# An attention kernel on one core: six products for the row maxima of a unit become four, and they are issued in another order

## What is computed

```python
qkv = (x @ w_qkv.T).reshape(B, N, 3, H, hd).transpose(2, 0, 3, 1, 4)   # 8 heads, hd = 24, g = 8
q3, q4, q5 = (q[..., :g], q[..., g:2 * g], q[..., 2 * g:])             # k and v the same way
x3 = merge(_attn(q4, concatenate([k3, k4], axis=2), concatenate([v3, v4], axis=2), scale))
x4 = merge(_attn(q5, concatenate([k3, k5], axis=2), concatenate([v3, v5], axis=2), scale))
x5 = merge(_attn(q5, concatenate([k4, k5], axis=2), concatenate([v4, v5], axis=2), scale))
out = concatenate([x3, x4, x5], axis=2) @ w_proj.T + b_proj            # _attn: softmax(q k^T * scale) v
```

## Time and profile before

| | |
|---|---|
| median of 3 runs | 1871.29 us (1869.54 to 1872.24) |
| profiled execution, its own time | 1873.42 us |
| its span, first to last instruction | 1871.7 us |
| busy in the span | PE 96%, DVE 80%, ACT 78%, POOL 67% |
| attention stage | from about 354 to 1429 us |
| mean granted TensorE clock | 0.98 |

### The profile page before, as it was taken

The page is one execution under the profiler, slowest core; times in us unless marked ns, Lnnn a source line. Parts: engine busy times, 40 slices in busy tenths (PEclk is TensorE's granted clock), DMA queues, the critical chain, the costliest instruction groups (busy, mean ns, idle before and its releaser), DMA issues. The chain is left out here.

```text
span 1871.7 us, 59000 instructions
## 1 busy us (share of the span) xinstructions
PE 1789.6 (96%) x20032; PEld 1015.8 (54%) x20032; DVE 1495.4 (80%) x3674; ACT 1462.8 (78%) x2983; POOL 1252.7 (67%) x2306
## 2 busy tenths in 40 slices
PE   5999999599999999999999999999994999999999
PEld 3677777244444444444444444444442777777776
DVE  6887878689999999999999999999994555555554
ACT  4666666288889888988898889988884777777775
POOL 4777776467777777777777777777753565666661
PEclk9999999699999999999999999999997999999999
DMA  7344442144444444444444444444441333333332
GB/s 192 90 112 112 112 112 68 35 81 87 89 88 89 89 88 88 90 88 90 88 88 88 90 89 89 87 92 88 88 79 28 72 70 68 70 67 71 65 74 54
DMA packets 503935, 159.49 MB, mean 85 GB/s; under 512 B 452176, under 2 KB 503120, under 8 KB 503888
## 3 DMA queue, kind: packets, MB, share of 16 engines
q1 hardware_dynamic: 503888, 158.90, 40.0%
HBM read 37.26 MB, written 12.48 MB: 27 GB/s over the span
## 5 line engine op out<-in xcount | busy, mean ns | idle before, releaser
L749 DVE TENSOR_REDUCE tops<-p_maxa 128x6 f32<-128x762 f32 x512 | 482.4, 942 | 63.2 <-PE p_maxa L587 61.4
L658 PE MATMUL p_o<-probs,vn 127*32 127x256 f32 x6144 | 410.8, 385 | 0.3 <-DVE att L777 0.3
L583 PE MATMUL p_s<-qm,kt 32*128 32x256 f16 x3072 | 399.9, 276 | 1.0 <-ACT probs L704 0.4
L701 ACT ACTIVATE probs<-p_s 128x512 f32<-128x512 f32 x512 | 305.4, 596 | 108.9 <-PE p_s L583 95.1
L751 DVE TENSOR_REDUCE tops<-p_maxb 128x4 f32<-128x508 f32 x512 | 345.9, 676 | 0.0
L707 ACT ACTIVATE probs<-p_s 128x512 f32<-128x512 f32 x512 | 309.0, 603 | 0.0
L704 ACT ACTIVATE probs<-p_s 128x512 f32<-128x512 f32 x512 | 304.6, 595 | 0.3 <-PE p_s L583 0.2
L587 PE MATMUL p_maxa<-kt,qt 24*128 24x256 f16 (+1 forms) x2048 | 283.9, 250 | 17.4 <-DMA qt<-qk 8.8
L1056 DVE TENSOR_TENSOR gel_lo<-gel,gel_hi 128x512 f16<-128x512 f32 x192 | 151.0, 787 | 168.9 <-ACT gel_hi L1028 168.7
L802 POOL TENSOR_TENSOR qk<-raw,one 128x384 f16<-128x384 f32 x128 | 105.7, 826 | 220.8 <-ACT raw L725 220.8
L583 PEld LDWEIGHTS p_s<-qm,kt 32*128 32x128 f16 x3072 | 135.2, 91 | 182.6 <-issue 164.8
(11 more groups left out here) (213 smaller groups left out, 4556.9 us busy)
## 6 DMA issues: line engine op xcount, KB each, us to landing
xt_a<-in_xt SPq DMA_DIRECT2D x32, 512.0 KB, 4.4
xt_b<-in_xt SPq DMA_DIRECT2D x64, 256.0 KB, 5.2
out<-out_sb SPq DMA_DIRECT2D x32, 336.0 KB, 2.6
xt<-hx SPq DMA_TRANSPOSE x128, 2.4
kt<-qk SPq DMA_TRANSPOSE x128, 2.8
qt<-qk SPq DMA_TRANSPOSE x128, 2.4
qm<-qk SPq DMA_TRANSPOSE x128, 2.7
yt<-ay SPq DMA_TRANSPOSE x128, 2.3
```

The lines of the kernel that those rows point to most:

```text
L583: return nc.tensor.matmul(o, kt[full(j), r, kind, g, :], qm[full(j), r % 2, versions, g, :], start=True, stop=True, skip_group_check=True)
L658: last = nc.tensor.matmul(p_o[32 * j:32 * j + 32, blocks, :], vn[0:NP, r, src:src + 32], probs[0:NP, r % 2, QUAD * g + j, kind * 256:(kind ...
L701: nc.scalar.activation(probs[:, r % 2, h + 1, 0:512], p_s[1][:, :, :].rearrange("p x n -> p (x n)"), ACT.Exp, scale=SCALE).then_inc(act_e1 ...
L749: nc.vector.tensor_reduce(top[:, q, pair, 4:10], p_ma[:, 0:6, 0:NP], AX.X, ALU.max, negate=True).then_inc(dve_ma[u], 1)
```

## The change

A unit now issues four maxima products instead of six. c and d each issue one product of 256 columns into `p_maxb` and one of 384 columns into `p_maxa`, whose two banks have one writer each (c blocks 0 to 2, d blocks 4 to 6). `p_maxb` is the bank with two writers: c's half opens the unit, with the wait for `dve_mb[u-1]` (and in unit 2 those for `kt` and `qt`) ahead of all else, and d's half comes near its end, after a wait for `pe_fc`. Among the scores, the second half of `p_s5` closes the unit. `pe_ma` counts two per unit, and the waits on it are doubled. The reduction of `p_maxa` reads two pieces of three blocks. The three minima become two instructions.

```diff
-                        ready(pe_ma[1], seen(i + 1))
+                        ready(pe_ma[1], seen(2 * (i + 1)))
...
+                if has_m and u == 2:
+                    pe.wait_ge(dma_k, seen(16 * (bm + 1)))
+                    pe.wait_ge(dma_q, seen(16 * (bm + 1)))
+                if has_m:
+                    pe.wait_ge(dve_mb[u - 1], seen(i + 2 if u < 3 else i + 3))
+                    maximum(p_mb[:, 0:2, :], c, 0, slice(0, 2)).then_inc(pe_fc[u], 1)
                 if has_s:
                     if u == 0:
                         pe.wait_ge(dma_qm, seen(16 * (i + 1)))
                     pe.wait_ge(act_e1[u - 1] if u else act_e1[3], seen(i + 1 if u else i))
                     score(p_s[1][:, 0:2, :], b, 0, slice(0, 2))
-                if has_m:
-                    if u == 2:
-                        pe.wait_ge(dma_k, seen(16 * (bm + 1)))
-                        pe.wait_ge(dma_q, seen(16 * (bm + 1)))
-                    pe.wait_ge(dve_ma[u - 1], seen(i + 2 if u < 3 else i + 3))
-                    maximum(p_ma[:, 4:5, :], c, 1, slice(2, 3)).then_inc(pe_fc[u], 1)
                 if has_s:
                     pe.wait_ge(act_e5[u - 1] if u else act_e5[3], seen(i + 1 if u else i))
                     score(p_s5[:, 0:2, :], a, 2, slice(1, 3)).then_inc(pe_half[u], 1)
                 if has_m:
-                    maximum(p_ma[:, 0:2, :], d, 0, slice(0, 2))
+                    pe.wait_ge(dve_ma[u - 1], seen(i + 2 if u < 3 else i + 3))
+                    maximum(p_ma[:, 0:3, :], c, 1, slice(0, 3)).then_inc(pe_ma[u], 1)
+                    maximum(p_ma[:, 4:7, :], d, 1, slice(0, 3)).then_inc(pe_ma[u], 1)
                 if has_s:
                     score(p_s[1][:, 2:4, :], b, 1, slice(0, 3, 2)).then_inc(pe_s1[u], 1)
-                if has_m:
-                    maximum(p_ma[:, 2:4, :], d, 1, slice(0, 2))
-                    pe.wait_ge(pe_fc[u], seen(bm + 1))
-                    maximum(p_ma[:, 5:6, :], d, 1, slice(2, 3)).then_inc(pe_ma[u], 1)
-                    pe.wait_ge(dve_mb[u - 1], seen(i + 2 if u < 3 else i + 3))
-                    maximum(p_mb[:, 0:2, :], c, 0, slice(0, 2))
                 if has_s:
                     pe.wait_ge(act_e0[u - 1] if u else act_e0[3], seen(i + 1 if u else i))
                     score(p_s[0][:, 0:2, :], a, 0, slice(0, 2))
+                    score(p_s[0][:, 2:4, :], a, 1, slice(0, 3, 2)).then_inc(pe_s0[u], 1)
                 if has_m:
-                    maximum(p_mb[:, 2:4, :], c, 1, slice(0, 2)).then_inc(pe_mb[u], 1)
+                    pe.wait_ge(pe_fc[u], seen(bm + 1))
+                    maximum(p_mb[:, 2:4, :], d, 0, slice(0, 2)).then_inc(pe_mb[u], 1)
                 if has_s:
                     pe.wait_ge(pe_half[u], seen(2 * i + 1))
                     score(p_s5[:, 2:4, :], b, 2, slice(1, 3)).then_inc(pe_half[u], 1)
-                    score(p_s[0][:, 2:4, :], a, 1, slice(0, 3, 2)).then_inc(pe_s0[u], 1)
...
-                    dve.wait_ge(pe_ma[u], seen(bm + 1))
-                    nc.vector.tensor_reduce(top[:, q, pair, 4:10], p_ma[:, 0:6, 0:NP], AX.X, ALU.max, negate=True).then_inc(dve_ma[u], 1)
+                    dve.wait_ge(pe_ma[u], seen(2 * (bm + 1)))
+                    nc.vector.tensor_reduce(top[:, q, pair, 4:10].rearrange("p (e k) -> p e k", e=2),
+                                            p_ma[:, :, :].rearrange("p (e k) n -> p e k n", e=2)[:, :, 0:3, 0:NP],
+                                            AX.X, ALU.max, negate=True).then_inc(dve_ma[u], 1)
...
-                    nc.vector.tensor_tensor(low[0], four[:, :, :, 0], four[:, :, :, 1], ALU.min)
-                    nc.vector.tensor_tensor(low[1], four[:, :, :, 2], fifth, ALU.min)
-                    nc.vector.tensor_tensor(low[2], four[:, :, :, 3], fifth, ALU.min).then_inc(dve_min, 1)
...
+                    nc.vector.tensor_tensor(low[:, 0], fourth[:, :, :, 0], fourth[:, :, :, 1], ALU.min)
+                    nc.vector.tensor_tensor(low[:, 1:3], fifth[:, 0:2], fifth[:, 2:3].broadcast_to([128, 2, QUAD, 2]), ALU.min).then_inc(dve_min, 1)
```

More of the change, by code:

```diff
@@ L762, in body @@
                     got = top[:, (r + 1) % 2]
-                    four = got[:, :, 0:8].rearrange("p a (e k) -> p a e k", e=2)
-                    fifth = got[:, :, 8:10]
-                    low = [slots((r + 1) % 2, 256 * x, HEADS)[:, :, 24].rearrange("p (a e) -> p a e", e=2) for x in range(3)]
-                    nc.vector.tensor_tensor(low[0], four[:, :, :, 0], four[:, :, :, 1], ALU.min)
-                    nc.vector.tensor_tensor(low[1], four[:, :, :, 2], fifth, ALU.min)
-                    nc.vector.tensor_tensor(low[2], four[:, :, :, 3], fifth, ALU.min).then_inc(dve_min, 1)
+                    fourth = got[:, :, 0:4].rearrange("p a (e k) -> p a e k", e=2)
+                    fifth = got[:, :, 4:10].rearrange("p a (e k) -> p k a e", e=2)
+                    low = slots((r + 1) % 2, 0, NQ)[:, :, 24].rearrange("p (x a e) -> p x a e", x=3, e=2)
+                    nc.vector.tensor_tensor(low[:, 0], fourth[:, :, :, 0], fourth[:, :, :, 1], ALU.min)
+                    nc.vector.tensor_tensor(low[:, 1:3], fifth[:, 0:2], fifth[:, 2:3].broadcast_to([128, 2, QUAD, 2]), ALU.min).then_inc(dve_min, 1)
                 maxima(i, r, 2)
```

## The result

The changed kernel takes 1960.51 us (median of 4 runs, 1959.1 to 1960.66) against 1870.41 us for the kernel before in the same comparison: the ratio is 1.0479, with a 95% interval of 1.0461 to 1.0497. That is 90 us slower; forecast were 64 us and 1935 us, with 1910 to 1965 as the range. The profiled execution has a span of 1958.9 us.

What follows compares the result with a forecast made beforehand. PE and DVE bound the kernel together; the wait at the head makes a serial PE-DVE-PE hand-over, so a block takes 8.61 us against 8.10; 0.51 x 125 = 64 us, about 1935 us, range 1910 to 1965.

Steps and rivals of the forecast that it cites:

- R: Time from a unit's opening on PE to DVE's start on it: forecast 0.50 us, bounds 0.45 and 0.61, today 0.61.
- the sum: The new block added up unit by unit: DVE starts at 0.50, releases PE at 2.10; unit 1 the same.
- close at 0.60: Every unit on PE: last two products start 0.40 after the opening, the unit closes at 0.60, 0.07 us less than today.
- the release of 0.05 us: After DVE's p_maxb reduction: PE's waiting product starts 0.05 us after its end, part of the 1.60 from DVE's start to release.
- the waits at the ends of loop trips: Today's waits contained in the mean of 8.10 us a block; the new slack should swallow them.
- 8.61: Forecast period of one new attention block in us, 8.60 to 8.63, which is +0.51 against 8.10.
- the mean of 8.10: Attention block period before the change: 395 reductions of p_maxb in 800 us at four a block, 8.10 us each.
- the sentence on hidden DMAs: At unit 2: dma_k and dma_q are awaited 4.2 us after unit 0's opening instead of 3.5, so that wait gets more room.
- PE's shorter units: Rival 1, at each unit's opening: dve_mb comes in time, block 7.52 us, time 1798 us; chance 0.04.
- The clock: Rival 4: PE idle some 1.1 of 8.6 us lowers its clock; one block in ten spoiled gives about 2000 us; chance 0.05.
- Rival 3: First halves bring DVE nothing, something holds the minima: R 0.61 or above, period 8.85 to 8.95, 1965 to 1977 us; chance 0.09.
- Held minima: Part of rival 3: something holds DVE's minima, costing 0.05 to 0.1 us in unit 2.

Runs made afterwards that it cites:

- the first edit: The changed kernel with both unit 2 waits, dma_k and dma_q, moved before the last eight records of output products ahead of unit 2: 1969.8 us, ratio 1.0535.

## Why the prediction held, and where it was short

**The cause is as forecast.** `dve_mb` at the head puts the buffer freed last in front of everything, DVE cannot start before PE is released, and the two alternate. The run with the wait alone (+127 us) and the one with the product put back (68 of 90 us regained) show it from both sides.

**Terms that held.** R was 0.50 by the sum and 0.51 in unit 1 (904.75 - 904.24), 0.50 in unit 2 (906.95 - 906.45). The 384-column product, which no row of before showed, has a record of 0.330 against the estimate of 0.33. A unit closes 904.83 - 904.24 = 0.59 after its opening in unit 1 and 0.57 in unit 2, against 0.60. Units 2 and 3 last 908.55 - 906.45 = 2.10 and 910.85 - 908.55 = 2.30, against 2.12 and 2.31. Unit 0 lasted 912.97 - 910.85 = 2.12 against 2.10. The two 384-column products fill 904.25 to 904.68; the later one has a record of 0.32 and starts at 904.36, 0.12 behind the opening, as taken. By the rule of the Trainium skill ("TensorE: Matmul & The Clock Gate", Part 3, The mechanism) it would have been about 0.21, an estimate from the 0.12 and the 0.09 of a load; the trace does not agree.

**A term that was wrong and did not show.** Units 0 and 3 do not close at 0.60: unit 0 takes 911.50 - 910.85 = 0.65 and in the block shown 0.75, unit 3 takes 0.70. In both DVE's release comes as late or later, so the openings behind them did not move. That unit 3 came out right is in part luck: PE reaches the next opening after 0.70 + 1.60 = 2.30, just when DVE releases it.

**The terms that were too small.** The step that failed in size is the release of 0.05 us used for every unit, and with it the sentence that the waits at the ends of loop trips would be swallowed and leave nothing. First, unit 1 lasts 906.45 - 904.24 = 2.21 where the sum had 2.10, because unit 2 opens 0.15 after the reduction in each of the 91 blocks, for the semaphore instruction described above: 0.08 to 0.1 us a block. Second, in two of the four blocks of a loop trip, the block shown among them, the first score product of unit 0 starts 0.18 to 0.20 behind the opening (902.23 against 902.03), where it is 0.10 in the other two (the next block); it holds the `p_maxa` products, R is 0.61 there (902.64 - 902.03), and unit 0 lasts 2.20 or 2.21 instead of 2.12. One unit 3 in four is longer by 0.09 too. In the blocks that run before and after the loop the first score product is not later than 0.10, so this belongs to the loop; what in it takes the time is not shown. Four openings of unit 0, from 902.03 on, lie 8.82, 8.73, 8.72 and 8.89 apart, a mean of 8.79, where the steady block takes 8.72: 0.07 us a block. With 0.02 of rounding these are the 0.18 us between 8.61 and 8.79, and 0.18 x 125 is 22 of the 25 us missing; the other 3 are not traced.

**What the mean of 8.10 held.** The 0.07 us by which it lies above the 8.03 of one block is, in the trace of before, the queries' DMA at unit 2 (2.30 us on average against 2.22), and not DVE. The new slack did swallow that: in the kernel after `qt` has landed 0.57 to 0.75 us before unit 2 opens. The delays of the loop in units 0 and 3 came in its place. So the sentence on hidden DMAs was right for the kernel after and blind to what it meant for the one before: that `dma_q` "gets more room" means that it had none.

**The rivals.** PE's shorter units did not decide: its own work, 0.65 + 0.59 + 0.57 + 0.70 in the units and 5.12 beside them, is 7.6 us in a period of 8.79. The clock did not fall: the granted clock was 1.00, the 2.4 GHz level, in the stretch with PE busy 0.89 of the time, so the swing that the Trainium skill describes ("TensorE: Matmul & The Clock Gate", A second HAM failure mode: psum-queue depth-cycling) did not occur in this trace. Rival 3 came in part: R was 0.61 in unit 0 of two blocks in four, for the late score product and not for a late first half. Held minima did not come: they end before unit 2's reduction starts, at 906.55 + 0.22 = 906.77 against 906.95.

## What to carry to other kernels

Before a wait is moved to the head of a group, ask which of the buffers is freed last, and by whom: here DVE frees `p_maxa` first and `p_maxb` 0.6 us later, and an order of products that needs them the other way round costs more than 4 x 0.08 us of shorter units can give. Where two engines hand buffers to and fro, write one period out as times from opening to opening, with both engines in it; the busy shares of 96% and 80% said nothing of this ring. And look for the second bound that a chain already touches, a DMA that lands just as it is needed, since it decides what an improvement ahead of it is worth. Last, where a product opens a serial ring, count the semaphores that it waits for: here the waits beyond the first cost 0.09 us in every block.

## What was not expected of the hardware

- Between a reduction's recorded end and the weight load that waits for it lie 0.053 us where the load has no other wait, and 0.117 where the product waits for two or three semaphores: the trace then has a semaphore instruction of 0.051 us ahead of the load. From that load to its product lie 0.031, in the other units 0.004.
- From SP's issue of the transposing DMA of `qt` to its landing it took 2.40 to 2.43 us, and the maxima product that stood waiting for it started 0.09 later, 2.49 to 2.52 after the issue, in the kernel before, with the opening product late, and with the short reduction. The output product of the first edit at unit 2 started 2.54 to 2.57 after it.
- The handover of a bank between two strips hardly depends on the size of the first product. After one of 256 columns the second writer starts at 0.34 (904.58 - 904.24), where I had taken 0.40; after one of 128 columns the products behind the wait started at 0.35 (902.10 to 902.45).
- One of the two 384-column products starts together with the opening (904.25), the other 0.11 later, although c's is issued first and d's strip is the free one. It looks as if d's overtook it: of the two weight loads in the packed trace the one without a wait, d's, starts at 904.251, the one that waits for `dve_ma`, c's, at 904.253. The records of the products do not name the strip, so this is read from the loads and the times.
